# A shared expert's batches spread by halves over two cycles each, and its last three batches placed behind the last expert tile

## What is computed

```python
# x is the sum of the input and the attention's output
def _L0_ffn_ref(x, gate_w, expert_bias, sw1, sb1, sw2, sb2, rw1, rb1, rw2, rb2):
    xf = x.reshape(-1, d)                               # after a layer norm
    sh = gelu(xf @ sw1 + sb1) @ sw2 + sb2               # shared expert, every row
    logits = xf @ gate_w.T + expert_bias
    topv, topi = top_k(logits, 2)                       # 7 routed experts
    w = softmax(topv)
    combine = sum(one_hot(topi, 7) * w[..., None], axis=1)
    h = gelu(einsum('td,edh->eth', xf, rw1) + rb1[:, None, :])
    out_e = einsum('eth,ehd->etd', h, rw2) + rb2[:, None, :]
    routed = einsum('te,etd->td', combine, out_e)
    return (sh + routed).reshape(b, s, d)
x = x + _L0_ffn_ref(_layernorm(x), ...)
```

## Time and profile before

| | |
|---|---|
| device time, median of 3 runs | 864.57 us (864.25 to 865.86) |
| the profiled execution's device time | 863.94 us |
| its span | 862.1 us |
| PE busy | 769.9 us, 89% of the span |
| DVE busy | 615.8 us, 71% |
| ACT busy | 477.2 us, 55% |
| POOL busy | 259.5 us, 30% |
| cycles, gate(0) to the first tile's transposes | 550.2 to 693.7 us |
| tiles | 693.7 to 822.7 us |
| end, no TensorE work | 822.7 to 862.1 us |

### The profile page before, as it was taken

One profiled execution on the slowest core, in us unless ns is written; L12 is line 12 of the kernel. 1 busy time (PEld: TensorE's weight loads), 2 busy tenths in 40 slices (PEclk: granted clock), 3 DMA queues, 4 the chain that ended last, 5 costly groups with the idle time before them and its releaser, 6 DMA issues. The chain is left out here.

```text
span 862.1 us, 18204 instructions
## 1 busy us (share of the span) xinstructions
PE 769.9 (89%) x6177; PEld 537.0 (62%) x6177; DVE 615.8 (71%) x1907; ACT 477.2 (55%) x720; POOL 259.5 (30%) x405
## 2 busy tenths in 40 slices
PE   4879878999999999999999997799999889999910
PEld 2768636666666666666665564556664489999910
DVE  5567377888888888888888851576674457777745
ACT  2334304666666666666666673464554267777700
POOL 1111011121112111111112110267567326666620
PEclk9989956999999999999999999799998999999975
DMA  4899783553356334553355633555422445555369
GB/s 120 239 349 333 256 234 96 141 141 106 102 152 167 109 99 129 165 141 93 104 158 162 202 114 142 153 167 183 142 86 80 141 132 159 160 161 161 124 246 381
DMA packets 74486, 140.73 MB, mean 163 GB/s; under 512 B 14504, under 2 KB 34624, under 8 KB 74222
## 3 DMA queue, kind: packets, MB, share of 16 engines
q1 hardware_dynamic: 64434, 119.52, 45.6%
q0 software_dynamic: 9792, 19.54, 6.9%
q10 hardware_dynamic: 172, 0.56, 0.3%
HBM read 85.70 MB, written 56.78 MB: 165 GB/s over the span
## 5 line engine op out<-in xcount | busy, mean ns | idle before, releaser
L721 DVE CUSTOM_DVE_ANT_0 sums<-pS,near 128x512 bf16<-128x512 f32 x512 | 329.5, 688 | 54.2 <-PE pS L783 45.8
L754 ACT ACTIVATE prob<-pE 128x1024 f32<-128x1024 f32 x256 | 248.5, 1022 | 154.8 <-PE pE L808 154.7
L808 PEld LDWEIGHTS pE<-bandT,place 64*128 64x128 f32 x2048 | 167.1, 190 | 12.5
L808 PE MATMUL pE<-bandT,place 64*128 64x244 f32 (+2 forms) x2048 | 164.4, 272 | 0.0
L783 PE MATMUL pS<-k_st,q_st 48*128 48x512 f32 x512 | 140.1, 479 | 10.6 <-DVEq L707 7.7
L783 PEld LDWEIGHTS pS<-k_st,q_st 48*128 48x128 f32 x512 | 63.8, 194 | 120.4 <-DVE nmax L721 88.9
L822 PE MATMUL pC<-prob,v_aug 128*32 128x512 f32 x1024 | 135.8, 604 | 1.0 <-ACT ctx_sb L762 1.0
L800 PE MATMUL pE<-q_st,k_st 62*128 62x512 f32 x512 | 115.3, 405 | 1.8 <-DMA q_st<-negated_maxima 1.1
L1055 POOL DMA_INDIRECT expert_rows<-rb,xr x76 | 84.1, 1106 | 57.0 <-DVE rb L1233 45.1
L1039 POOL DMA_INDIRECT routed_rows<-xr,slot_i x64 | 65.4, 1022 | 46.1 <-DVE slot_i L1167 27.4
L1510 PE MATMUL pD<-w2p,hT 128*128 x456 | 63.5, 289 | 0.4 <-DVE hT L1226 0.4
(11 more groups left out here) (169 smaller groups left out, 1040.4 us busy)
## 6 DMA issues: line engine op xcount, KB each, us to landing
xr<-routed_rows SPq DMA_DIRECT2D x38, 258.0 KB, 2.9
q_parts<-qk SPq DMA_DIRECT2D x16, 512.0 KB, 5.4
k_parts<-qk SPq DMA_DIRECT2D x16, 512.0 KB, 5.1
q_st<-q_parts SPq DMA_DIRECT2D x64, 128.0 KB, 2.8
k_st<-k_parts SPq DMA_DIRECT2D x64, 128.0 KB, 2.9
ctx<-ctx_sb SPq DMA_DIRECT2D x32, 256.0 KB, 2.7
near<-bias_by_distance SPq DMA_DIRECT2D x16, 448.0 KB, 5.0
xr<-expert_rows SPq DMA_DIRECT2D x12, 512.0 KB, 7.4
```

What stands on the lines that cost most here:

```text
L721: dve.tensor_tensor_reduce(sums[:, r % 4], pS[:, unit % PS], near[:, hg % 2, j, lead:lead + S], -1.0, BIG, ALU.add, ALU.min, nmax[:, j, t: ...
L754: act.activation(prob[:, par, 2 * step:2 * step + 2], pE[:, 2 * (step % 2):2 * (step % 2) + 2], ACT.Exp).then_inc(exp_done, 1)
L808: ins = pe.matmul(pE[:, bank + side, a:z], place[rows, half], bandT[rows, (quad // 2) % 2, pair, part, lead:lead + z - a], start=False, st ...
```

## The change

The shared expert is moved, its arithmetic stays. Batches 0, 1 and 2 are spread over two cycles each: in an odd cycle i, for b = i // 2, `shared_up(b, 0)` behind the gate and `shared_up(b, 1)` with `turn_shares(b)` behind `turn_rows`; in the next even cycle the first half of `shared_down(b)` behind the gate and the second half behind `turn_rows`. Batch 3 begins in cycle 7 and is finished, with batch 4, between the cycles and the tiles. Batches 5, 6 and 7 stand behind the last tile, and their `add` among the `gather_add`s. On ACT, `turned(i + 1)` is now ahead of `weights_hi`, and `hidden(b, 1)` and `shares(b)` are at the end of an odd cycle. x2T has 5 buffers, by a table; the first three even batches after batch 0 reuse one and wait for the `shared_up` that reads it last. combine_p has 5 buffers. To make room, three small tables of `tile_table` lie in wst and the late denominators in the tile of the early ones. The diff gives first the tiles, then DVE's list, ACT's and PE's.

```diff
-XB = 2
+EARLY = 3
+CB = 5
+TILES_FROM = 5
+X2_SLOT = (0, 1, 0, 2, 1, 3, 0, 4)
...
-        den = sb("den_late", [P, DW], F32)
+        den = g["den_early"]
...
-        x2T = sb("x2T", [P, XB, MC, S], F32)
+        x2_own = sb("x2T", [P, 5, MC, S], F32)
...
                 for i in range(B):
                     if 1 <= i < B - 1:
                         residual(i + 1)
-                    if i >= 2:
-                        add(i - 2)
+                    if i >= 3 and i % 2 == 1:
+                        add((i - 3) // 2)
                     choose(i)
...
                 tile_table()
-                add(B - 2)
-                add(B - 1)
+                for b in range(EARLY, TILES_FROM):
+                    add(b)
...
                 for b in range(B):
                     gather_add(b)
+                    if b % 2 == 1 and TILES_FROM + b // 2 < B:
+                        add(TILES_FROM + b // 2)
...
                 def turned(b):
                     for c in range(MC):
                         act.wait_ge(s["xT2_mm"], 2 * b + c + 1)
-                        if b >= XB:
-                            act.wait_ge(s["u_mm"], 2 * (b - XB) + 2)
-                        act.activation(x2T[:, b % XB, c], pX[:, 0, c], ACT.Copy).then_inc(s["xT2"], 1)
+                        if b in (2, 4, 6):
+                            act.wait_ge(s["u_mm"], b)
+                        act.activation(x2T(b)[:, c], pX[:, 0, c], ACT.Copy).then_inc(s["xT2"], 1)
...
                 for i in range(B):
                     gate(i)
-                    if i >= 1:
-                        hidden(i - 1, 0)
+                    if i % 2 == 1:
+                        hidden(i // 2, 0)
                     soft(i)
-                    if i >= 1:
-                        hidden(i - 1, 1)
                     if i + 1 < B:
                         normalise(i + 1, 0)
-                    if i >= 1:
-                        shares(i - 1)
+                        turned(i + 1)
                     if i < NR:
                         for k in (2 * i, 2 * i + 1):
                             weights_hi(k)
                     if i + 1 < B:
-                        turned(i + 1)
                         normalise(i + 1, 1)
-                hidden(B - 1, 0)
-                hidden(B - 1, 1)
-                shares(B - 1)
+                    if i % 2 == 1:
+                        hidden(i // 2, 1)
+                        shares(i // 2)
+                for b in range(EARLY + 1, TILES_FROM):
+                    hidden(b, 0)
+                    hidden(b, 1)
+                    shares(b)
...
+                for b in range(TILES_FROM, B):
+                    hidden(b, 0)
+                    hidden(b, 1)
+                    shares(b)
...
-                def shared_down(b):
+                def shared_down(b, halves=(0, 1)):
...
                 for i in range(B):
                     gate(i)
-                    if i >= 1:
-                        shared_up(i - 1, 0)
+                    if i % 2 == 1:
+                        shared_up(i // 2, 0)
+                    elif i >= 2:
+                        shared_down(i // 2 - 1, (0,))
                     turn_logits(i)
-                    if i >= 1:
-                        shared_up(i - 1, 1)
                     if i + 2 < B:
                         out_projection(i + 2)
-                    if 1 <= i < B - 1:
-                        turn_shares(i - 1)
                     rank(i)
                     if i + 1 < B:
                         turn_rows(i + 1)
-                        if i >= 1:
-                            shared_down(i - 1)
-                shared_up(B - 1, 0)
+                    if i % 2 == 1:
+                        shared_up(i // 2, 1)
+                        turn_shares(i // 2)
+                    elif i >= 2:
+                        shared_down(i // 2 - 1, (1,))
+                shared_up(EARLY + 1, 0)
...
-                turn_shares(B - 2)
-                shared_down(B - 2)
-                shared_up(B - 1, 1)
-                turn_shares(B - 1)
-                shared_down(B - 1)
+                shared_up(EARLY + 1, 1)
+                shared_down(EARLY)
+                turn_shares(EARLY + 1)
+                shared_down(EARLY + 1)
...
+                for m in range(2):
+                    shared_up(TILES_FROM, m)
+                for b in range(TILES_FROM, B):
+                    turn_shares(b)
+                    if b + 1 < B:
+                        for m in range(2):
+                            shared_up(b + 1, m)
+                    shared_down(b)
```

More of the change, by code:

```diff
@@ L899, in finish @@
         pad_at = sb("pad_at", [1, NE], I32)
-        over = sb("over", [P, NE, STEPS], F32)
+        spare = wst[:].rearrange("p k c d -> p (k c d)")
+        over = spare[:, 0:NE * STEPS].rearrange("p (e s) -> p e s", e=NE)
+        square = spare[:, NE * STEPS:NE * STEPS + NE * NE].rearrange("p (a b) -> p a b", a=NE)
+        ended = spare[0:1, D:D + NTP * NR].rearrange("p (i e) -> p i e", i=NTP)
         tiles_of = sb("tiles_of", [P, NE], F32)
         upto = sb("upto", [P, NE], F32)
-        square = sb("square", [P, NE, NE], F32)
-        ended = sb("ended", [1, NTP, NR], F32)
         line = sb("line", [1, 3, NTP], F32)
@@ L915, in finish, with x2T @@
         y_half = [rb[:, k].rearrange("p c s -> p (c s)").rearrange("p (k t d) -> p k t d", k=2, t=2) for k in range(2)]
+        def x2T(b):
+            return x2_own[:, X2_SLOT[b]]
         def up_bank(i, m):
@@ L1190, in tile_table @@
                     link(dve.tensor_copy(upto[:], counts))
-                    link(dve.tensor_tensor(over[:], upto[:].unsqueeze(2).to_broadcast([P, NE, STEPS]),
+                    link(dve.tensor_tensor(over, upto[:].unsqueeze(2).to_broadcast([P, NE, STEPS]),
                                            steps.unsqueeze(1).to_broadcast([P, NE, STEPS]), ALU.is_gt))
-                    link(dve.tensor_reduce(tiles_of[:], over[:], mybir.AxisListType.X, ALU.add))
-                    link(dve.tensor_tensor(square[:], below, tiles_of[:].unsqueeze(1).to_broadcast([P, NE, NE]), ALU.mult))
-                    link(dve.tensor_reduce(upto[:], square[:], mybir.AxisListType.X, ALU.add))
-                    link(dve.tensor_tensor(ended[:], tile_no.unsqueeze(2).to_broadcast([1, NTP, NR]),
+                    link(dve.tensor_reduce(tiles_of[:], over, mybir.AxisListType.X, ALU.add))
+                    link(dve.tensor_tensor(square, below, tiles_of[:].unsqueeze(1).to_broadcast([P, NE, NE]), ALU.mult))
+                    link(dve.tensor_reduce(upto[:], square, mybir.AxisListType.X, ALU.add))
+                    link(dve.tensor_tensor(ended, tile_no.unsqueeze(2).to_broadcast([1, NTP, NR]),
                                            upto[0:1, 0:NR].unsqueeze(1).to_broadcast([1, NTP, NR]), ALU.is_ge))
-                    link(dve.tensor_reduce(line[:, 0], ended[:], mybir.AxisListType.X, ALU.add))
-                    link(dve.tensor_tensor(spent, ended[:],
+                    link(dve.tensor_reduce(line[:, 0], ended, mybir.AxisListType.X, ALU.add))
+                    link(dve.tensor_tensor(spent, ended,
                                            tiles_of[0:1, 0:NR].unsqueeze(1).to_broadcast([1, NTP, NR]), ALU.mult))
@@ L1332, in hidden @@
                     act.wait_ge(s["u_mm"], 2 * b + m + 1)
+                    if b == TILES_FROM:
+                        act.wait_ge(s["hlo"], NT)
                     if b >= 1:
@@ L1423, in gate @@
                     for c in range(MC):
-                        ins = pe.matmul(pX[0:NR, 0, 0], ga_f[:, c], x2T[:, b % XB, c], start=c == 0, stop=c == MC - 1)
+                        ins = pe.matmul(pX[0:NR, 0, 0], ga_f[:, c], x2T(b)[:, c], start=c == 0, stop=c == MC - 1)
                     ins.then_inc(s["g_mm"], 1)
@@ L1450, in turn_shares @@
                     pe.wait_ge(s["comb_done"], 3 * b + 3)
+                    if b == TILES_FROM:
+                        pe.wait_ge(s["ev_done"], 2 * NT)
                     if b >= 1:
@@ L1454, in turn_shares @@
                     for t in range(TT):
-                        ins = pe.transpose(flat[:, P * t:P * t + P], raw(combine_p[:, b % XB, t]), ident[:])
+                        ins = pe.transpose(flat[:, P * t:P * t + P], raw(combine_p[:, b % CB, t]), ident[:])
                     ins.then_inc(s["c_turn"], 1)
                 def shared_up(b, m):
+                    if b == TILES_FROM:
+                        pe.wait_ge(s["hhi"], 2 * NT)
                     if b >= 1:
@@ L1461, in shared_up @@
                     for c in range(MC):
-                        ins = pe.matmul(pU[:, m], w_sh[:, 0, c, P * m:P * m + P], x2T[:, b % XB, c],
+                        ins = pe.matmul(pU[:, m], w_sh[:, 0, c, P * m:P * m + P], x2T(b)[:, c],
                                         start=c == 0, stop=c == MC - 1)
                     ins.then_inc(s["u_mm"], 1)
-                def shared_down(b):
```

(3 more changed lines are left out.)

14 lines of the change are left out of this document (7 added, 7 removed).

## The result

The change takes 868.88 us (median of 20 runs, 865.33 to 874.34), the kernel before on the same chip 865.63 (20 runs, 861.78 to 870.52). The ratio is 1.0037, 95% interval 1.0019 to 1.0055: **slower by 0.37%**. That is +3.2 us, where the likeliest case had -0.4 and rival C, at half of its price, +2.8. It lies in the range, but the change is slower, and it was expected to come out even. The profiled execution has 866.91 us and a span of 865.1, against 862.1 before.

A forecast was written before the change was run, and what follows sets the result against it. TensorE was taken to bound the cycles (17.17 us each), with idle TensorE in the end. First part -6.5 us and end +6.1 gave -0.4 on 863.94, thus 863.5, on the median 864.1 us; range 858.0 to 869.0.

The forecast's parts named there:

- the likeliest case: Whole kernel: cycles gain 6.5 us, the end pays back 6.1, -0.4 in all, 864.1 us, the same as before.
- rival C: Even cycles: half clock outlasts its cover through out_projection, 3.5 us each, end 1.5 more; 870.7, half of it 867.4; chance 0.23.
- case A: The forecast itself: clock falls in most even cycles, own range 861.5 to 866.5 us; chance 0.46.
- rival B: Cycles: the clock holds despite the gap, the 5.4 us is not lost, 858.7 us; chance 0.23.
- The end's order: End: TensorE waits 3.7 us for add(5) behind gather_add(1); the gather_adds end at 863.3 instead of 858.11, +5.2 us.
- Rival D: End: gathered rows come so late that DVE waits anyway, add(6) and add(7) cost 2 us, not 5.2; 860.9; chance 0.08.
- the chain to the tiles: Cycle 7 to the first tile: places, eight scatters, SP's loads and first tile were taken as unchanged.
- In cycle 7 only two pieces of down are left ahead of the gate, 2.7 less ... I charge 0.3.: Cycle 7 to the tiles: 2.7 us gained ahead of the gate, 0.3 (0 to 1.5) charged for one more shared_up.
- The idle 3.7 us ... begins warm: I take 0.9 of the 3.4.: End: TensorE's idle ahead of turn_shares(6) begins at full clock, so the clock's fall costs 0.9 us there.
- the upper bound that the prediction kept: End: half of the 6.8 us at half clock after the idle stretch is lost, 3.4 us.
- I take 1.8 for each.: Gaps in cycles 2, 4, 6: the clock's fall costs 1.8 us each, 5.4 for three; from 0 up to 3.5 each.
- a part of each passes while TensorE waits: Even cycles: stretches at half clock, 6.9 and 3.4 us in the rows, partly fall in TensorE's waits, hence 1.8 each.

The follow-up runs named there:

- the five idle products: The change plus five 128x256 products on TensorE, read by nobody, ahead of shared_down's first half in cycles 2, 4 and 6: 862.50 us, ratio 0.9961.
- the execution with idle products: The change plus nine 128x256 products, read by nobody, between shared_down(5) and turn_shares(6) in the end, none in the cycles: 868.74 us, ratio 1.004.
- the fastest kernel: The change plus five 128x256 idle products before shared_down's first half (cycles 2, 4, 6), end adds behind gather_add(0), (4), (6): 852.72 us, ratio 0.9838.
- the slower group: Runs with all kernels slower (before 876.21 us); the change with the counts' product moved ahead of turn_shares(3) took 876.58 us, ratio 1.0027.

## Why the prediction was right and wrong

**Right: the bound and the waits.** TensorE's work went out of the cycles, and ScalarE's order took its place: 2.24 to 2.35 us of idle ahead of `shared_down` (2.6 said), released by `cTs`, in cycles 2, 4 and 6. Odd intervals were 12.4 (13.0), even ones at full clock 15.9 (16.5). The clock fell in all three even cycles, as case A has it (0.50 from 583 to 586 and from 613 to 616, 0.56 from 645 to 650), and rival B didn't happen; the five idle products come near to what it would have been, 128.8 us to the first tile, even below B's. The end's order is right in mechanism: TensorE waits for `add(5)` behind `gather_add(1)`. An estimate for the order alone: 30.8 us in the execution with idle products, less 1.0 for its slow `shared_up` and 0.4 for its slow `turn_shares`, leaves 29.4 against 24.8, so 4.6, where 5.2 was said. Rival D fails on the same rows: behind the first rows DVE waited for TensorE, not for rows.

**Wrong: the price of the clock, and one link of the chain to the tiles.** It is rival C's mechanism, and this is why the sign came out on the other side. The terms against three profiles of the same cycles (change in us over the kernel before; the second has only the adds moved, the third only idle products in the end):

| stretch | forecast | the change | adds moved | idle products in the end |
|---|---|---|---|---|
| gate(0) to the transposes of batch 2 | -0.4 | -1.6 | +0.3 | +0.1 |
| to the transposes of batch 7 | -3.1 | -1.5 | -5.7 | -5.4 |
| to the first tile | -3.0 | -0.2 | -0.3 | -0.7 |
| together | -6.5 | -3.3 | -5.7 | -5.9 |

1. *"In cycle 7 only two pieces of down are left ahead of the gate, 2.7 less ... I charge 0.3."* This step failed in all three. The gate did come 2.7 to 3.1 us sooner, but the way from the rank of batch 7 to the counts grew by 2.8 in the first two (in the third by 1.2, with 1.1 more ahead of the rank). The chain to the tiles was called unchanged, scatters and SP's loads; the link of the counts was overlooked, and the moved work stands ahead of them in TensorE's list. Of the 2.8 some 1.2 remain at full clock (4.1 us against 2.9) and 1.6 are the half clock. That the first tile hangs on the counts is read from the chain of waits; the run that moved them didn't confirm it. With that `shared_up` at full clock the whole way was 32.9 to 33.2 in three profiles, where 33.3 follows from the forecast, and 35.6 in a fourth.
2. *"The idle 3.7 us ... begins warm: I take 0.9 of the 3.4."* Starting at full clock (1.00 from 822.0 to 830.8) did not help; from 834 to 840 it was 0.50. The end's `gather_add` stretch grew by 8.5 us, of which 4.6 are order, so the clock took some 3.9, more than the upper bound that the prediction kept. What lies behind the last `gather_add` was 0.9 shorter, which leaves +7.7. Three more profiles with this order of adds and no idle products in the end have +6.6, +8.6 and +10.0, and one of the slower group +9.9: 6.1 was too little in all.
3. *"I take 1.8 for each."* Three falls, 5.4 in all, against intervals at full clock of 72.4 us: measured 10.1 in the change's profile, 5.9 and 6.2 in the two others. In cycle 4 of the change it is 4.4 (20.25 less 15.89): the pieces of `shared_down`, the logits and `out_projection` (6.00 for 4.11) all run at half clock, one behind the other. The step that failed there is "a part of each passes while TensorE waits": TensorE is gapless through 613 to 622, and nothing is absorbed. In cycle 2 it is 4.4 too (20.28 less the 15.88 of the fastest kernel), but 1.5 of these come from the fall ahead of the transposes of batch 2, a wait that the prediction saw (0.4) and didn't price for the clock. In cycle 6 it is 1.3. With only the adds moved, cycle 4 took 17.63, a price of 1.7. So 1.8 is the low end of what was seen, 4.4 the high end.

The intervals came out well in two profiles by luck: at full clock they would take 72.4 us where 75.5 was said, and these 3.1 us hid what the clock cost above the 5.4. The gain in cycle 1 is no more certain: +0.3 and +0.1 with the same list, so the -1.6 is the execution's.

In the change's own profile, against the forecast: +2.8 for cycle 7, +1.6 in the end and +1.6 in the intervals are partly met by -1.2 in cycle 1. That is +4.8 on a forecast of -0.4, and with -1.1 ahead of gate(0), which varied from 549.1 to 557.0 between profiles, and -0.3 in the tiles it gives the +3.0 of the spans. The ratio of the timings is +3.2 us.

## What to carry to other kernels

Price a gap on TensorE by what runs behind it until the clock is back, across the boundaries of stages and from more than one profile, and look for a serial chain in that stretch (here the counts for the padding). When work is moved into another engine's idle time, write down where its consumer stands in that engine's list: two lines of order in the end were worth 5.6 us of its length, part of it because the clock held (two `shared_up` took 3.60 us for 5.65). A fill of idle products is a cheap test for whether the clock is the cause, if its length is taken from a row and no DMA sets the end of the gap.

## What the runs showed of the hardware

- A gap of 2.24 or 2.35 us ahead of `shared_down`, behind a gate that ran at its normal 1.88 us, ended with the clock at 0.50 in cycles 2 and 4 of the change; gaps of 0.37 to 0.80 us didn't. In the end waits of 1.44, 1.78 and 1.81 us left the products behind them at full clock, and 2.57, 2.67 and 4.36 did not. Just behind a gap of 1.78 us with 0.88 more following it, it fell too (with two batches behind the tile four products took 2.07).
- Between these lengths the same gap can end either way. Behind 2.26 to 2.28 us ahead of the transposes of batch 2 these took 1.97 us in four of twelve profiles and 1.09 in eight. Behind 2.20 to 2.30 us ahead of the rank of batch 7 one `shared_up` took 1.96 us in four profiles, 3.54 to 3.61 in four others and something between in three.
- The clock's return differs between executions of the same instructions: the interval of cycle 4 was 20.25, 17.63, 17.64 and 18.80 us in four profiles with the same cycles.
- A float32 product with 512 columns took 0.88 to 0.91 us (nine in 7.89, five in 4.56), one with 256 columns 0.45 to 0.48 (nine in 4.05, five in 2.42), and the profile counts two matmuls for each. The first fill was sized as if it were one.
